# dx in a PSUM bank, one up bank, the second layer's convolution on TensorE, its state products summed in pairs

## The reference, cut to what matters

```
x_in, z = x @ W_in.T split                       # x_in: 256 channels
xc   = causal depthwise conv over 4 tokens of x_in, + bias
xs   = silu(xc)
dt, B, C = small projections of xs;   delta = softplus(dt)
for each token: h = exp(delta*A) * h + delta*B*xs        # 16 states a channel
y    = sum over the 16 states of h*C,  + D*xs,  times silu(z)
ffn  = sum over 8 experts of cw * (silu(x@Wg) * (x@Wu)) @ Wd
out  = gated product of the two, + x
```

## Time and profile before

| | |
|---|---|
| Median, three runs | 956.6 us |
| The profiled execution, its time | 957.64 us |
| Its span on the core | 955.8 us |
| VectorE busy | 809.0 us (85%) |
| TensorE busy | 827.9 us (87%) |
| GpSimd busy | 521.8 us (55%) |
| ScalarE busy | 427.4 us (45%) |

### The profile page before, as it was taken

One profiled execution on the slowest core, in us unless ns is written; L12 is line 12 of the kernel. 1 busy time (PEld: TensorE's weight loads), 2 busy tenths in 40 slices (PEclk: granted clock), 3 DMA queues, 4 the chain that ended last, 5 costly groups with the idle time before them and its releaser, 6 DMA issues. The chain is left out here.

```text
span 955.8 us, 10838 instructions
## 1 busy us (share of the span) xinstructions
PE 827.9 (87%) x2368; PEld 403.0 (42%) x2368; DVE 809.0 (85%) x1127; ACT 427.4 (45%) x691; POOL 521.8 (55%) x336
## 2 busy tenths in 40 slices
PE   2947998899799979977799998899986999888997
PEld 1413443444344434333354443454443554444454
DVE  4389648956995698649999999999999999999995
ACT  2633455445445535455244633345553345533331
POOL 0067617652764365426654566654756455576773
PEclk9977999899899989889999999999999999999999
DMA  8253155313533255147554466565746544555861
GB/s 233 66 157 113 45 187 151 112 54 97 141 117 85 77 160 164 34 121 179 152 161 146 124 175 157 156 143 139 171 126 166 145 137 139 153 155 159 183 166 42
DMA packets 85275, 128.76 MB, mean 135 GB/s; under 512 B 7304, under 2 KB 27984, under 8 KB 85232
## 3 DMA queue, kind: packets, MB, share of 16 engines
q1 hardware_dynamic: 85232, 128.32, 49.6%
HBM read 124.82 MB, written 3.47 MB: 134 GB/s over the span
## 5 line engine op out<-in xcount | busy, mean ns | idle before, releaser
L880 POOL TENSOR_TENSOR product<-state,CB 128x512 f32<-128x512 f32 x128 | 203.6, 1592 | 193.4 <-DVE state L604 192.6
L604 DVE TENSOR_TENSOR_SCAN state<-decay,drive 128x512 f32<-128x512 f32 x192 | 274.0, 1429 | 5.0 <-ACT decay L1153 1.3
L1349 PE MATMUL bank<-XH,wh 128*128 128x512 f32 x256 | 193.1, 754 | 3.8 <-issue 2.0
L1153 ACT ACTIVATE decay<-delta,negA 128x510 f32<-128x510 f32 x192 | 135.5, 714 | 111.9 <-DVE state L604 111.6
L1463 PE MATMUL bank<-xw,wu 128*128 128x512 f32 x256 | 137.5, 619 | 51.0 <-DVE hid L734 50.3
L597 DVE TENSOR_TENSOR drive<-dx,CB 128x512 f32<-128x512 f32 x192 | 166.2, 867 | 9.4 <-DMA CB<-crow 6.2
L1411 PE MATMUL bank<-hid,wd 128*128 128x512 f32 x256 | 152.9, 681 | 9.5 <-ACT hid L1160 9.5
L1160 ACT ACTIVATE hid<-bank,early 128x512 f32<-128x512 f32 x128 | 87.3, 685 | 138.9 <-PE bank L1411 128.2
L1199 ACT ACTIVATE sg<-bank 128x512 f32<-128x512 f32 x128 | 75.9, 593 | 149.9 <-PE bank L1351 135.1
L1471 PE MATMUL bank<-hid,wd 128*128 128x512 f32 x256 | 133.2, 602 | 0.0
L1364 PE MATMUL bank<-product,early 128*128 128x512 f32 x232 | 117.2, 595 | 1.4 <-DVE xd L740 1.4
(11 more groups left out here) (158 smaller groups left out, 928.3 us busy)
## 6 DMA issues: line engine op xcount, KB each, us to landing
CB<-crow SPq DMA_DIRECT2D x256, 256.0 KB, 4.6
CB<-crow SPq DMA_DIRECT2D x64, 512.0 KB, 4.9
cwb<-cwrow SPq DMA_DIRECT2D x32, 256.0 KB, 5.8
wu<-W_dram SPq DMA_DIRECT2D x8, 256.0 KB, 5.8
wd<-W_dram SPq DMA_DIRECT2D x8, 256.0 KB, 6.6
wu<-Wu_dram SPq DMA_DIRECT2D x8, 256.0 KB, 4.1
xw<-Wg_dram SPq DMA_DIRECT2D x8, 256.0 KB, 4.3
wd<-Wd_dram SPq DMA_DIRECT2D x8, 256.0 KB, 4.9
```

The costliest lines, as they stand in the source:

```text
L604: v.tensor_tensor_scan(state[:, c % RING, :], decay[:, c % RING, :], drive[:, c % 2, :], 0.0, ALU.mult, ALU.add).then_inc(state_ready.sem, 1)
L880: ins = p.tensor_tensor(dst, state[:, c % RING, :], CB[:, c % ROWS, 0, :], ALU.mult)
L1153: a.activation(by_batch(decay[:, c % RING, :])[:, :, 1:], by_batch(delta[:, m, :])[:, :, 1:], ACT.Exp, scale=negA[:, c:c + 1]).then_inc(de ...
L1349: t.matmul(dst, wh[:, e, ws], XH[:, :], start=True, stop=False)
```

## The change: what it does

- **dx** is one tile in PSUM bank 6 (`DX_BANK`) for both layers, instead of two tiles in SBUF. `form_dx` for the second channel tile moves from GpSimd (slot 9) to VectorE, ahead of the drive of chunk 16 (slot 15).
- **One up bank**: `up1(u-1)` waits until unit u-2's hid is formed; before, it was unit u-3's. `down1(u-3)` goes ahead of `gate1(u)` in the slot.
- **Convolution**: `fold_conv` multiplies W_in's x half by each tap on GpSimd, once. Then xi0 and xi1 are four products each on shifted views of the padded xn^T, in one bank. ScalarE reads that bank twice (tanh, and half of it), and the taps on VectorE, the copies to xpad and the first taps go. "xi1" moves from slot 15 to slot 17, behind "z0"; xs0 and xs1 come earlier.
- **Sums**: for each pair of chunks GpSimd makes two products and adds them; TensorE sums 16 entries a turn instead of 29.
- Four small DMAs bring the taps, in front of the W2 loads.

```diff
-HEAD1 = {..., 12: "xi0", 13: "tap01 logits", 14: "lmax", 15: "tap02 lexp xi1",
-         16: "tap03 z0 tz0", 17: "th0 sz0", 18: "xs0", 19: "tap11", 20: "row0 tap12", 21: "z1 tz1 tap13 soft1", 22: "sz1 th1",
-         23: "xs1", 24: "dt0 soft2", ...}
+HEAD1 = {..., 12: "xi0", 13: "logits", 14: "lmax", 15: "lexp",
+         16: "xs0 z0 tz0", 17: "sz0 xi1", 19: "xs1", 20: "row0", 21: "z1 tz1 soft1", 22: "sz1",
+         24: "dt0 soft2", ...}
+PAIR = 2
+ENTRIES = C1 // PAIR
+SUMS1 = [max(CHUNKS1[PAIR * e + PAIR - 1] + SUM_LAG1, LATE + 1) for e in range(ENTRIES)]
...
+        dx = bank[DX_BANK][:, :]
...
+            def form_dx(at, m, u, drives):
+                dve.wait_ge(delta_ready.sem, at(delta_ready, m + 1))
+                dve.wait_ge(drive_ready.sem, at(drive_ready, drives))
+                v.tensor_tensor(dx, delta[:, m, :], xs[:, u, :], ALU.mult).then_inc(dx_ready.sem, 1)
...
-                v.tensor_tensor(drive[:, c % 2, :], dx[:, m, :], CB[:, c % ROWS, 1, :], ALU.mult).then_inc(drive_ready.sem, 1)
+                v.tensor_tensor(drive[:, c % 2, :], dx, CB[:, c % ROWS, 1, :], ALU.mult).then_inc(drive_ready.sem, 1)
...
             def multiply1(at, c):
...
+                e = c // PAIR
+                cs = CB[:, c % ROWS, 0, :]
+                if c % PAIR == 0:
+                    pool.wait_ge(summed.sem, at(summed, max(e - PRODS + 1, 0)))
+                    p.tensor_tensor(product[:, e % PRODS, :], state[:, c % RING, :], cs, ALU.mult).then_inc(state_used.sem, 1)
+                else:
+                    pool.wait_ge(group_ready.sem, at(group_ready, e))
+                    p.tensor_tensor(addend, state[:, c % RING, :], cs, ALU.mult).then_inc(state_used.sem, 1)
+                    pool.wait_ge(state_used.sem, at(state_used, c + 1))
+                    p.tensor_tensor(product[:, e % PRODS, :], product[:, e % PRODS, :], addend, ALU.add).then_inc(group_ready.sem, 1)
...
+            def fold_conv():
...
+                for k in range(KC - 1):
+                    p.tensor_tensor(w_cv[:, k, :], w_cv[:, k, :], w_x, ALU.mult).then_inc(cv_step.sem, 1)
...
                 if name in ("xi0", "xi1"):        # ScalarE
...
+                    a.activation(th[:, :], hb[:, :], ACT.Tanh, bias=col1("bconv", m), scale=0.5).then_inc(th_ready.sem, 1)
+                    a.activation(conv[:, m, :], hb[:, :], ACT.Identity, bias=col1("bconv", m), scale=0.5).then_inc(head_read.sem, 1)
...
+                if name in ("xi0", "xi1"):        # TensorE
...
+                    for k in range(KC):
+                        taps = w_cv[:, k, :] if k < KC - 1 else w_in1[:, 0:J1 * 128]
+                        last = t.matmul(by_batch(hb[:, :]), taps[:, 128 * m:128 * m + 128], XNP[:, :, k:k + L], start=(k == 0), stop=(k == KC - 1))
...
             def up1(i, u):
-                pe.wait_ge(hid_ready.sem, hid_ready.at1(i, u - 1))
-                t.matmul(bank[UP_BANK + u % 2][:, :], ...)
+                pe.wait_ge(hid_ready.sem, hid_ready.at1(i, u))
+                t.matmul(bank[UP_BANK][:, :], ...)
...
             def slot1(i, u, head=None, j=None, late=None):
...
+                if u > LAG1:
+                    down1(i, u - LAG1)
                 gate1(i, u)
+                if u > 0 and late:
+                    late(u)
+                if u == LAG1:
+                    down1(i, u - LAG1)
                 if u > 0:
                     up1(i, u - 1)
-                if u > 0 and late:
-                    late(u)
-                if u >= LAG1:
-                    down1(i, u - LAG1)
                 for e in now(SUMS1, u):
                     sum_entry(i, e)
```

More of the change, by code:

```diff
@@ L65 @@
          25: "less ln"}
-HEAD1 = {6: "stat1", 7: "var1", 9: "xn", 11: "xnT", 12: "xi0", 13: "tap01 logits", 14: "lmax", 15: "tap02 lexp xi1",
-         16: "tap03 z0 tz0", 17: "th0 sz0", 18: "xs0", 19: "tap11", 20: "row0 tap12", 21: "z1 tz1 tap13 soft1", 22: "sz1 th1",
-         23: "xs1", 24: "dt0 soft2", 25: "row1 rest0 soft3", 26: "dt1 less0", 27: "cwT rest1", 28: "less1 ln", 29: "xr"}
+HEAD1 = {6: "stat1", 7: "var1", 9: "xn", 11: "xnT", 12: "xi0", 13: "logits", 14: "lmax", 15: "lexp",
+         16: "xs0 z0 tz0", 17: "sz0 xi1", 19: "xs1", 20: "row0", 21: "z1 tz1 soft1", 22: "sz1",
+         24: "dt0 soft2", 25: "row1 rest0 soft3", 26: "dt1 less0", 27: "cwT rest1", 28: "less1 ln", 29: "xr"}
 XW_SLOT = 30
@@ L74 @@
 PRODS = 3
[L75 to L85, removed]
+PAIR = 2
+ENTRIES = C1 // PAIR
+SUMS1 = [max(CHUNKS1[PAIR * e + PAIR - 1] + SUM_LAG1, LATE + 1) for e in range(ENTRIES)]
+SUMS1 = [max(at, CHUNKS1[N - 1] + SUM_LAG1 + 2) if PAIR * e >= N else at for e, at in enumerate(SUMS1)]
 FINISH_Y0 = CHUNKS1[N - 1] + SUM_LAG1 + 1
@@ L1286, in head_product @@
             def head_product(rows, weights, rhs):
-                t.matmul(hb[0:rows, :], weights, rhs, start=True, stop=True).then_inc(head_ps.sem, 1)
+                dst = hb[0:rows, :] if len(rhs.shape) == 2 else by_batch(hb[0:rows, :])
+                t.matmul(dst, weights, rhs, start=True, stop=True).then_inc(head_ps.sem, 1)
             def head0(name, j):
@@ L1325, in head1 @@
                     transposes(hb, lambda k: xn[:, k, :], head_ps)
-                if name in ("xi0", "xi1", "z0", "z1"):
-                    m = J1 * "xz".index(name[0]) + int(name[-1])
-                    head_product(128, w_in1[:, 128 * m:128 * m + 128], XNT[:, :])
+                if name in ("xi0", "xi1"):
+                    m = int(name[-1])
+                    if m == 0:
+                        pe.wait_ge(cv_ready.sem, cv_ready.at0(0, 1))
+                    for k in range(KC):
+                        taps = w_cv[:, k, :] if k < KC - 1 else w_in1[:, 0:J1 * 128]
+                        last = t.matmul(by_batch(hb[:, :]), taps[:, 128 * m:128 * m + 128], XNP[:, :, k:k + L], start=(k == 0), stop=(k == KC - 1))
+                    last.then_inc(head_ps.sem, 1)
+                if name in ("z0", "z1"):
+                    m = J1 + int(name[-1])
+                    head_product(128, w_in1[:, 128 * m:128 * m + 128], XNT)
                 if name == "logits":
@@ L1331, in head1 @@
                         kind, tile = k // TT, k % TT
-                        last = t.matmul(hb[:, E * k:E * k + E], XNT[:, 128 * tile:128 * tile + 128],
+                        last = t.matmul(hb[:, E * k:E * k + E], xn_tile(tile),
                                         w_r1[:, E * kind:E * kind + E], start=True, stop=True)
@@ L1461, in up1 @@
                     pe.wait_ge(wu_in.sem, wu_in.at0(0, 16 * E))
[L1462 to L1463 removed]
+                pe.wait_ge(hid_ready.sem, hid_ready.at1(i, u))
+                t.matmul(bank[UP_BANK][:, :], wu[:, e, 128 * f:128 * f + 128], xw[:, e % 2, :], start=True, stop=True).then_inc(up_ps.sem, 1)
             def down1(i, u):
```

111 lines of the change are left out of this document (51 added, 60 removed).

## The result

The changed kernel takes 974.95 us (median of 4 runs, 971.67 to 977.96), the kernel before beside it 959.07 (4 runs, 956.46 to 963.60): ratio 1.0157, 95% interval 1.0113 to 1.0200. The profiled execution took 973.61 us, its span is 971.8 against 955.8 of before: 16.0 us more, where 9.7 were forecast.

A forecast was written before the change was run, and what follows sets the result against it. VectorE was taken to set the pace in layer 1, TensorE in layer 0. Head turns +9, last turn +2, layer 0 -4.5 and +2.2, start +1 gave +9.7 on 957.6: 966 us, range 946 to 976.

The forecast's parts named there:

- scans (adds and xw, less present holds): Layer-1 head turn: GpSimd adds and token weighing hold scans, +11.9 us, less 2.6 us of the scans' present holds.
- other held instructions: Layer-1 head turn: xs and the rounding step lie beside longer GpSimd products; 1.3 us of holds, an estimate.
- dx of the second tile: One more VectorE instruction, 0.6 us free and 1.65 held, taken as 0.7 us a turn.
- Part 1: dx in PSUM frees the drives from holds: 5.8 us less a layer-1 turn, 1.5 less a turn in layer 0.
- the rival that they would not be freed: dx in PSUM does not free the drives, and adds start after the scan: 985 us, chance 0.04.
- Part 2: Six taps leave VectorE in each head turn: 7.7 us less.
- Part 3: GpSimd's 16 adds a turn instead of 3 hold VectorE's scans: +11.9 us per head turn, bounds 5 and 18.
- Part 4: One up bank and convolution on TensorE make gg late in slots 12, 13 and 17: +7.8 us a head turn, bounds 0 and 10.
- the third rival: Waits bring TensorE's clock down, a few us at 1.2 GHz, 4 us per head turn: total 980 us, chance 0.08.
- Layer 0's last turn: TensorE is the bound in its middle: -1.5 us from dx, +5.1 for products, some 1.4 covered by a wait: +2.2.
- The first rival: TensorE's three waits fall where scans would be held anyway or other VectorE work covers them: 948 us, faster, chance 0.22.
- Part of it: Rival: waits half as long or adds at the low bound: 954 us, 950 to 961, no change, chance 0.17.

The follow-up runs named there:

- 29 sums: The changed kernel with three GpSimd adds a turn and 29 identity products on TensorE, instead of 16 and 16: 969.58 us, ratio 1.0129 to the kernel before.
- only dx: The kernel before with dx in PSUM and one up bank, down ahead of gate; taps on VectorE and 29 sums kept: 954.89 us, ratio 0.9959.

## Why the prediction was right, and what in it was off

The direction (slower) and the mechanism hold: one up bank takes TensorE's lead, gg waits for it in slots 13, 14 and 18, and what drives and taps save goes into waits and into scans behind adds. 974.95 lies in the range of 946 to 976, at its upper edge, 9 us above the 966 of the sum. Term by term, for a head turn of layer 1:

| term | forecast, us | second head turn, us |
|---|---|---|
| drives | -5.8 | -5.1 |
| taps | -7.7 | -7.9 |
| scans (adds and xw, less present holds) | +9.3 | +5.3 |
| other held instructions | -1.3 | +1.7 (xn alone) |
| dx of the second tile | +0.7 | -0.3 |
| gg's waits | +7.8 | +11.2 |
| loop's edge | 0 | +1.9 |
| sum | +3.0 | +6.8 (turn: +7.4) |

- **Part 1, drives: right.** All 192 lie at 657 to 693 ns, which the earlier trace rows of hid had shown, and the rival that they would not be freed is refuted. For layer 0 it was mis-sized: -1.5 us a turn forecast, -3.6, -2.5 and -2.8 measured, and 13 us up to layer 1 where dx is the only change. The forecast took one hold of 1 us ahead of xn; TensorE's wait for xn in turn 2 fell from 5.7 to 2.8 us.

```profile
248.82 3.50 DVE L510 TENSOR_SCALAR xn<-xt,mv,rstd 128x128 f32<-128x128 f32 x4
252.37 1.12 PE L1296 MATMUL bank<-early,xn 128*128 128x128 f32 x4 [2.79 <-DVE xn L510]
```

  In the kernel before, the drive ahead of xn took 1.69 us, the one ahead of it 0.67, and xn 4.13. Now all drives are short and xn takes 3.50: 1.0 and 0.6 are seen there. The rest comes from the scan and the drive some steps earlier (a scan of 2.02 us at 247.45 before). One held instruction was priced where there were several in a row.
- **Part 2, taps: right** to 0.2 us.
- **Part 3, adds: over-sized.** Scans rose by 5.3 us where +9.3 stood. In the last turn, where nothing else hides them, they rose from 43.3 to 53.5 us: +10.2 for 16 adds and the weighing of tokens, that is 0.6 a pair; the drives gave back 10 (32 x 326 ns), and the turn is +0.5 where +2 stood. The rows of that turn, before and then after:

```profile
L604 DVE TENSOR_TENSOR_SCAN state<-decay,drive 128x512 f32<-128x512 f32 x32 | 43.3, 1355 | 0.0
L597 DVE TENSOR_TENSOR drive<-dx,CB 128x512 f32<-128x512 f32 x32 | 31.5, 988 | 0.2 <-DVE dx L590 0.2
```
```profile
L616 DVE TENSOR_TENSOR_SCAN state<-decay,drive 128x512 f32<-128x512 f32 x32 | 53.5, 1674 | 0.0
L609 DVE TENSOR_TENSOR drive<-bank,CB 128x512 f32<-128x512 f32 x31 | 20.4, 662 | 1.1 <-DMA CB<-crow 1.0
```

In head turns it costs half of that; I read this as adds that end while gg waits, before the next scan starts, which no run takes apart.
- **Part 4, waits: right in place, under-sized.** Slots 13, 14 and 18 wait 3.21, 1.70 and 3.49 us where 2.3, 2.0 and 3.5 stood: 8.4 for 7.8. Three others were not foreseen: 1.24 and 0.72 in slots 11 and 12, and 0.88 at slot 0. The first follows the wait of 5.81 us and the half clock: a part of the third rival came true, in a place that it did not name. The adds lengthen that wait of TensorE: it ends with hid behind xn, and xn in slot 9 takes 5.06 us beside GpSimd's pairs. With 29 sums, and with only dx, it takes 3.03, and TensorE waits 2.80. The second is no matter of the clock: slot 12 waits 0.7 us with only dx too, behind a stretch at full clock. The run with dx alone shows the other half of the miss: slots with a sum, which the forecast left with 0.3 us of slack, wait too.
- **Layer 0's last turn: right in number by luck**, +2.0 for +2.2, as a larger loss against a larger gain. Without the convolution it takes 101.5 us (taps back on VectorE) or 104.4 (dx in layer 0 only), against 110.3 before. So the convolution costs 8 to 11: 5.1 were counted for its products; the wait for sz0, which only the head turns had been charged with, is 3.5; and behind it the first three products take 4.36 us instead of 2.84. With xi1 in slot 18, where that wait is 1.5 us, the cost is 5 (dx in PSUM in layer 0 only, with the convolution and without).

```profile
368.44 4.36 PE L1346 MATMUL bank<-XNP,w_cv 128*128 128x512 f32 x6 [3.53 <-DVE sz L708]
```

- **Start:** +1 forecast, -0.1 measured.

So the sum was short by 6: head turns +22.2 where +9 stood, layer 0 -7.0 where -1.3 stood (start with it), the last turn +0.5 where +2 stood.

The first rival (the lead covers the waits) is refuted by gg's 36 us. "Part of it" has its place in the scans, which cost half of their price.

The rule of the Trainium skill (SBUF — State Buffer, Who interferes with whom) that a VectorE instruction with two SBUF inputs and a GpSimd one that reads SBUF lock each other out, and that one with at most one SBUF input does not, is borne out by both sides: the same add takes 1357 ns beside drives that read PSUM and 1623 beside drives that read SBUF, and the drive 664 and 1044 (the kernel with dx in SBUF and two up banks). It is a lock and not a share: in the earlier trace rows a product starts 0.16 us into a drive, and the drive still takes 0.66 us, while the product ends 1.14 behind it. The rule excepts the two-port modes of VectorE, among whose instructions the section counts TENSOR_SCALAR, and the prediction left that out. It bears on xn, which has one SBUF tensor and yet is held: the four take 1.11 us at the start of the kernel before and 3.1 to 4.2 us in its turns.

## What to carry to other kernels

- A change of several parts is a sum only if each part's cost lies on the same engine as its gain. Here, by the ratios, dx alone is -4 us, the convolution +17, the pairs +45, and together they are +15: the pairs need dx in PSUM, and dx in PSUM takes the bank that gave TensorE its lead. Build each part alone, and ask of each in which stage it pays; the best version here is one part in one of two layers.
- Before giving up a second PSUM bank, count for each slot what stands in the queue behind the product that now waits, not only for the slots that grow: with only dx, where no slot of TensorE grows, gg waited 29 us in the head turns, half of it in waits of 1.1 us and less.
- A step moved behind another read of its bank waits for that reader's slot. Where the same order list serves a turn with another bound (here layer 0's last turn), price it there again.

## What the runs showed of the hardware

**The clock behind a wait.** In the kernel before, TensorE stood 2.94 us for hid in slot 9 and its next product took 1.12 us, at the full 2.4 GHz. In the changed kernel it stood 5.81 us there, and these windows of the three stretches (standing, behind it, later) give the granted clock as 1.00, 0.55 and 1.00; the second is mostly the lower level of 1.2 GHz:

```profile
603.00:607.00 4.00, 0.00 (x0) 0.00 (x0) 4.00 (x5) 0.07 (x1) 3.75 (x4) 1.00 0.77 149
607.00:610.80 3.80, 3.24 (x4) 1.46 (x5) 3.80 (x6) 0.00 (x0) 1.27 (x1) 0.55 0.76 189
610.80:616.00 5.20, 5.20 (x19) 2.99 (x18) 3.96 (x6) 1.80 (x3) 2.56 (x2) 1.00 0.52 157
```

Where the clock falls, a wait costs twice, the second time on the engine that is late already. The length of the wait alone does not tell whether it falls. With only dx, TensorE stood 2.81 us ahead of slot 9's up product in the first head turn and 2.80 in the second; the granted clock behind it was 0.50 (457 to 459 us) and 1.00 (594 to 596 us), and gg of slot 11 then waited 2.05 and 0.23 us. So a fall there cost 1.8 us:

```profile
456.41 2.07 PE L1540 MATMUL bank<-xw,wu 128*128 128x512 f32 x2 [2.81 <-DVE hid L767]
463.03 0.69 DVE L759 SCALAR_TENSOR_TENSOR gg<-sg,bank 128x512 f32<-128x512 f32 x1 [2.05 <-ACT sg L1262]
593.76 1.12 PE L1540 MATMUL bank<-xw,wu 128*128 128x512 f32 x2 [2.80 <-DVE hid L767]
598.99 0.69 DVE L759 SCALAR_TENSOR_TENSOR gg<-sg,bank 128x512 f32<-128x512 f32 x1 [0.23 <-ACT sg L1262]
```

The Trainium skill (TensorE: Matmul & The Clock Gate, HAM oscillation — how this bites in real kernels) tells of the same for a product that waits on a transfer: TensorE falls back to the lower clock in the wait and starts the next piece there. The trace agrees for the wait of 5.81 us, with a wait for VectorE as the cause.

**The loop's edge.** At slot 6, where the loop over turns begins again, VectorE stands with nothing that the profile shows as a cause ahead of hid (L743): 3.49 us in the second head turn after, 1.60 in the one before, and 1.3 to 3.5 over all runs. What makes it longer was not tried.

```profile
586.11 0.69 DVE L743 TENSOR_TENSOR hid<-gg,bank 128x512 f32<-128x512 f32 x1 [3.49 <-issue]
```
